# Key and value stage of a four-stage transformer kernel: Pool's clears and bias additions later, constant rows by the scalar engine, last products reordered

## The chip, the cores and the metric

The kernel runs on one core of one Trainium2 chip. The metric is device time in microseconds (us) of one execution. All engines of the core work at once from separate instruction streams and meet at semaphores: PE (TensorE, matrix products, with PEld its weight loads), DVE (VectorE), ACT (ScalarE), POOL (GpSimd, called Pool in the text) and SP (SyncE, which here issues nearly all DMA transfers).

## The reference, cut to what matters

The input x has 8 batches of 256 rows with 512 columns (2,048 rows, which the kernel keeps as 16 tiles of 128 rows). Four blocks are added to it in turn:

```python
x = x + long_convolution(ctx, ctx, layernorm(x))
x = x + quantised_ffn(layernorm(x), w1, b1, w2, b2)
x = x + attention(layernorm(x), ctx, Wq, bq, gq, Wk_img, bk_img, gk_img, Wv_img, bv_img, Wo, bo)
x = x + experts(x)          # 16 routed experts, the best 2 of each row, and 2 shared ones
```

The change lies in the third block's first half. There, with 256 context rows in each batch,

```python
q = rms_norm(x_n @ Wq + bq, gq)          # x_n = layernorm(x)
k = rms_norm(ctx @ Wk_img + bk_img, gk_img)
v = ctx @ Wv_img + bv_img
out = softmax(q k^T / sqrt(32)) v @ Wo + bo          # 16 heads of 32
```

where `rms_norm(y, g) = y * rsqrt(mean(y*y) + 1e-6) * g` over 512 columns. x at this point is the output of the second block, whose last bias (b2) is added late: in the kernel that addition is a step of its own.

## The kernel before, in words

The program is a row of stages, each a `Block` with one hand-written instruction list for each engine; a stage ends when all five engines have come to its end, and the next begins at once on all of them. Four matter here: `stage_ffn` (second block), `stage_keys_values`, `stage_attention`, and the lists of semaphores between them.

`stage_keys_values` works through ten **items** in the order `ITEMS`: keys of batches 0 to 4, queries of batch 0, keys of batch 5, queries of batch 1, keys of batches 6 and 7. An item is one projection of 256 rows to 512 columns, transposed (four chunks of 128 columns by 256 rows), computed as three bf16 products (high by high, high by low, low by high), 48 matmuls in all. Beside the items run sixteen **value tiles** (12 matmuls of 512 columns each), given out by the table `VALUES`: two in each of rounds 1 to 4, one in rounds 5 to 8, two in rounds 9 and 10. In **round i** PE does `products(i)`, `sums(i-1)` (sums of squares of the item before, four matmuls with one column), the value tiles of the round, and `spread(i-1)` (the row scales put on all partitions by a product with a diagonal matrix); in rounds 3 and 5 also `turn_x` (eight transposes of normalised x for a query item). A round with two value tiles is called a two-value round here, the others one-value rounds.

What joins the engines in round i: ACT splits the next source (`split_source(i+1)`), adds the bias and squares the products of item i (`squares`, eight activations), then copies the high parts of values (`values_high`) and of the finished item (`high(i-1)`). Pool folds the squares from four chunks to one (`fold_halves`, two additions) and raises the row variances to the power -1/2 (`row_scale`). DVE does the low part of the next source, `row_variance(i-1)`, the diagonal matrix (`row_scales(i-1)`, line 1179), values with bias and their low parts, `normalise(i-1)`, `low(i-1)`. SP stores each finished key item as three transfers of 256 KB (`store`), or stacks a query item with twelve of 64 KB. So PE's `spread(i-1)` waits for a chain: PE's sums, DVE's variance, Pool's power, DVE's diagonal matrix.

Work that is not part of this chain has been put beside it:

- Pool begins the stage with `clear_retired` (line 98), which sets the 99 semaphores of earlier stages to zero, then fills the constant columns of `v_hi` and `v_lo`, then adds b2 to two x tiles (`add_bias2`, tiles 4 and 5) ahead of the first fold, and to two more after each of the folds 0 to 4.
- The b2 additions of x tiles 0 to 3 stand in `stage_ffn`, on Pool, after rounds 12 to 15 of that stage (line 1048).
- DVE sets the 32 constant rows of `kb` (rows 96 to 127 of the keys of batch 0: zeros, and two rows of ones) with two memsets at the start (lines 1425, 1427), and takes the statistics of x tiles (`x_stats`): 0 to 3 at the start, then two in each of rounds 1 to 6.
- DVE's subtractions that make the low parts of Wq and Wo (`split_weights`, line 1400) stand at the end of rounds 1 and 2.
- In round 10, where nothing is left but values (7,0), (7,1) and item 9, PE does values (7,0), then `spread(9)`, then values (7,1); ACT and DVE have the matching order.
- SP stores item 9 at the end of the stage; nobody waits for that store until the keys of batch 7 are loaded in the attention stage.

At the end of the stage SP waits for all other stores (line 1187 in the profile). The functions follow with their line numbers.

Of the kernel before, what the change touches and what calls it, by code (L numbers as in the profile page):

```python
# [10 lines left out]
F32 = mybir.dt.float32  # L11
# [59 lines left out]
class Kernel:  # L71
# [26 lines left out]
    def clear_retired(self, pool):  # L98

        for s in self.retired:  # L100
            pool.sem_clear(s)
# [682 lines left out]
def stage_ffn(k, scales, b1_parts, b2, ahead, quantised):  # L784
# [3 lines left out]
    with ExitStack() as ctx:  # L788
# [254 lines left out]
        def _(pool):  # L1043
            pool.memset(ahead.rows[:, :], 0.0).then_inc(rows_zeroed, 1)

            def add_bias2(t):
                pool.wait_ge(y_added, t + 2)
                pool.tensor_tensor(tile(t), tile(t), b2[:, :].unsqueeze(1), ALU.add)

# [133 lines left out]
def stage_keys_values(k, ahead, b2, qw, ow, vectors, ks, v_hi, v_lo, x_mean, x_rstd, qs, kb, k_hi, k_lo):  # L1183
# [3 lines left out]
    with ExitStack() as ctx:  # L1187
# [12 lines left out]
        x_var, tmp = (sb(f"kv_{n}", [P, NT], F32) for n in ("xvar", "tmp"))  # L1200
        psW = ctx.enter_context(nc.psum_tensor("ps_kw", [P, P], F32))
# [10 lines left out]
        q_stacked, kb_loaded, kb_set = sem("qst"), sem("kbl"), sem("kbs")  # L1212
        w_high, w_low, rows_turned, vectors_ready, dve_step = (sem(n) for n in ("wh", "wlo", "rt", "ve", "dve"))
        stat_done, x_var_ready, x_rstd_ready, x_biased = (sem(n) for n in ("sd", "xv", "xr", "xb"))
# [13 lines left out]
        FIRST = AHEAD * TPB  # L1228

        @block.gpsimd  # L1230
        def _(pool):
            k.clear_retired(pool)
            pool.memset(v_hi[:, :, :, HD:], 1.0)
            pool.memset(v_lo[:, :, :, HD:], 0.0)

# [8 lines left out]
            def add_bias2(first):  # L1244
                for t in range(first, min(first + 2, NT)):
                    pool.tensor_tensor(k.x[:, t, :], k.x[:, t, :], b2[:, :], ALU.add).then_inc(x_biased, 1)

            add_bias2(FIRST)
            for i in range(N):
# [4 lines left out]
                add_bias2(FIRST + 2 * (i + 1))  # L1254
# [6 lines left out]
        def _(sp):  # L1261
            def store(i):
                b, p = batch(i), i % 2
                done = k.last_stored if i == N - 1 else stacked[p]
                sp.wait_ge(k_low, i + 1)
                for j, part in enumerate((k_hi[p], k_lo[p], k_hi[p])):
                    target = ks[b:b + 1, j * HD:(j + 1) * HD, :, :, :].rearrange("o d h c s -> (o h) d (c s)")
                    sp.dma_start(target, part[:, :, :].rearrange("p c s -> p (c s)")).then_inc(done, 16)
# [10 lines left out]
            for i in range(N):  # L1279
# [14 lines left out]
        def _(act):  # L1294
# [43 lines left out]

            split_source(1)
            act.wait_ge(vectors_ready, 1)  # L1340
            for i in range(N + 1):
# [6 lines left out]
                for n, tile in enumerate(VALUES[i]):  # L1348
                    if n and i == N:
                        high(i - 1, (i - 1) % 2)  # L1350
                    values_high(*tile)
                if 0 < i < N:
                    high(i - 1, (i - 1) % 2)

        @block.vector
        def _(dve):
# [44 lines left out]

            def x_stats(t):
                if t >= FIRST:
                    dve.wait_ge(x_biased, t - FIRST + 1)
                dve.bn_stats(stats[:, t, :], k.x[:, t, :]).then_inc(stat_done, 1)
# [26 lines left out]
            for i in range(1, N + 1):  # L1432
# [9 lines left out]
                if FIRST + 2 * (i - 1) < NT:  # L1442
                    x_stats(FIRST + 2 * (i - 1) + 1)
                if i == N:
                    normalise(i - 1, p)
                    value_low(*tiles[0])
                    low(i - 1, p)
                    value(*tiles[1])
                else:
                    value_low(*tiles[0])  # L1450
                    for tile in tiles[1:]:
                        value(*tile)
                    normalise(i - 1, p)
                for tile in tiles[1:]:
                    value_low(*tile)
                if i < N:
                    low(i - 1, p)
# [1613 lines left out]
```

## Time and profile before

| | us |
|---|---|
| median of three runs | 1165.79 |
| lowest, highest | 1162.44, 1165.82 |
| the profiled execution's own time | 1165.67 |
| its span, first to last instruction | 1163.9 |
| mean granted clock of PE | 0.939 of full |
| `stage_keys_values` in the span | 375.15 to 500.20 |
| PE, DVE, ACT, Pool busy over the span | 91, 76, 60, 52 % |

The profile is one execution, with every instruction's start and duration. A row of the timeline has the start, the duration, the engine, the line of the kernel, the operation, what is written and read, and, in square brackets, how long the engine sat idle before it and whom it waited for. Instructions of one engine overlap by about 0.1 us, so durations add up to a little more than the time that passes; where it matters, distances from start to start are used. The granted clock is 1.00 at PE's full rate (2.4 GHz) and 0.50 at its lower one (1.2 GHz). Waits for PE and DVE in this stage are more telling than the shares over the whole span, since stages have different limits.

### The profile page before, as it was taken

Reading aid. Unit: us, or ns where it says so; the run is one execution under the profiler, and the core shown is the slowest. Engines: PE = TensorE matmul, PEld = TensorE weight load, DVE = VectorE, ACT = ScalarE, POOL = GpSimd, SP = SyncE. Lnnn points to the kernel's source line nnn. Section 1 sums busy time; section 2 is a strip of 40 time slices with the busy share of each in tenths; the row PEclk is TensorE's granted clock in tenths of the full one; section 3 lists DMA queues with packets and bytes.
Section 4 is the critical chain, followed back from the end, with each engine's and each line's share of the span. In section 5 each row is a group of like instructions: output and inputs, shape, how many; then the busy total and the mean of one; then the engine's idle time right before and its main releaser. Section 6 shows DMA issues by size and latency. Waiting matters only on the chain. (4 is left out here: it accounts for less than half of the span.)

```text
span 1163.9 us, 24928 instructions
## 1 busy us (share of the span) xinstructions
PE 1057.2 (91%) x9247; PEld 783.7 (67%) x9247; DVE 881.0 (76%) x1594; ACT 697.4 (60%) x1135; POOL 603.2 (52%) x637
## 2 busy tenths in 40 slices
PE   5999997689997899868999999698998799999997
PEld 5777775634443567547777776497675688888884
DVE  5489999779998988657888888498975455555548
ACT  4564773779985546457888876285454254454531
POOL 4444445434455543348788888222686255555520
PEclk9999999789999999978999999757999799999999
DMA  8573531869885123222222220195697467768879
GB/s 311 165 258 120 163 113 33 156 197 231 231 214 157 67 67 111 76 78 56 54 56 58 56 56 2 51 379 193 168 261 244 146 228 246 240 236 283 314 260 355
DMA packets 133706, 194.62 MB, mean 167 GB/s; under 512 B 67990, under 2 KB 70204, under 8 KB 132792
## 3 DMA queue, kind: packets, MB, share of 16 engines
q1 hardware_dynamic: 117256, 149.45, 42.3%
q0 software_dynamic: 8544, 24.68, 6.7%
q10 hardware_dynamic: 7792, 18.96, 5.2%
q8 instruction: 72, 1.18, 0.4%
q14 instruction: 42, 0.34, 0.1%
HBM read 127.47 MB, written 44.48 MB: 148 GB/s over the span
## 5 line engine op out<-in xcount | busy, mean ns | idle before, releaser
L470 PE MATMUL ps_y<-kv,toep 128*128 128x288 f32 x640 | 157.7, 409 | 4.6 <-DMA toep<-taps_padded 2.4
L470 PEld LDWEIGHTS ps_y<-kv,toep 128*128 128x128 f32 x640 | 122.2, 192 | 39.6 <-DMA toep<-taps_padded 3.5
L1679 POOL TENSOR_TENSOR vw<-at_pf,kw 128x1024 bf16<-128x1024 f32 x64 | 136.5, 2133 | 2.7 <-ACT kw L1739 2.7
L164 POOL TENSOR_TENSOR kv<-kx 128x1024 f32<-128x1024 f32 x32 | 60.6, 1893 | 87.2 <-DVE outT L524 40.2
L2665 POOL DMA_INDIRECT expert_results<-e_yo,target x47 | 70.1, 1491 | 55.5 <-ACT e_yo L2716 55.5
L1735 ACT ACTIVATE at_pf<-ps_st 128x1024 f32<-128x1024 f32 x64 | 65.5, 1024 | 39.7 <-PE ps_st L1875 36.2
L1786 DVE TENSOR_REDUCE at_negmax<-ps_s 128x4 f32<-128x1024 f32 x64 | 78.4, 1224 | 2.5 <-PE ps_s L1836 0.6
L1147 PEld LDWEIGHTS ps_eg<-e_xT,e_w 128*128 128x128 bf16 x1128 | 68.6, 100 | 14.6 <-DVE e_w L2770 2.2
L1147 PE MATMUL ps_eg<-e_xT,e_w 128*128 128x128 bf16 x1128 | 72.6, 222 | 3.7 <-DVE e_xT L2777 3.7
L1147 PE MATMUL ps_eu<-e_xT,e_w 128*128 128x128 bf16 x1128 | 72.8, 222 | 0.0
L2770 DVE COPY e_w<-expert_weights 128x4096 bf16 x47 | 57.7, 1227 | 19.0 <-issue 19.0
L2660 POOL DMA_INDIRECT e_rows<-token_rows,token x45 | 43.5, 968 | 51.2 <-PE ps_ex L2867 45.3
L2783 DVE SCALAR_TENSOR_TENSOR e_y<-ps_eu,e_bias,e_y 128x128 f32<-128x128 f32 x94 | 28.7, 347 | 54.2 <-PE ps_eu L1147 53.5
L1739 ACT ACTIVATE kw<-at_pf 128x1024 bf16<-128x1024 f32 x64 | 67.6, 1057 | 2.0
L1100 PE MATMUL ps_fH<-w1T,f_qaT 128*128 128x512 bf16 x256 | 64.1, 395 | 3.6 <-PEq L636 2.1
L1147 PEld LDWEIGHTS ps_eu<-e_xT,e_w 128*128 128x128 bf16 x1128 | 67.1, 100 | 0.0
L1780 DVE COPY qs<-ps_m 32x256 bf16<-32x256 bf16 x128 | 37.6, 294 | 36.6 <-PE ps_m L1848 33.5
L2732 ACT ACTIVATE e_xT<-ps_ex 128x512 bf16<-128x512 bf16 x47 | 28.1, 597 | 58.8 <-PE ps_ex L2867 58.8
L1116 PE MATMUL ps_fY<-w2T,f_qbT 128*128 128x512 bf16 x256 | 59.4, 387 | 4.2 <-DMA f_qbT<-f_qb 4.2
L494 DVE TENSOR_TENSOR prod<-ps_y,qx 128x1024 f32<-128x1024 f32 x32 | 39.2, 1224 | 25.5 <-ACT ps_y L417 25.5
L1147 PE MATMUL ps_ed<-e_parts,e_yhi 128*128 128x512 bf16 x188 | 55.9, 379 | 0.4 <-DVE e_ylo L2791 0.4
L2725 ACT ACTIVATE e_y<-ps_eg,e_bias 128x128 f32<-128x128 f32 x94 | 29.4, 364 | 39.6 <-PE ps_eg L1147 31.1
(444 smaller groups left out, 3055.4 us busy)
## 6 DMA issues: line engine op xcount, KB each, us to landing
e_parts<-down_parts SPq DMA_DIRECT2D x47, 512.0 KB, 4.6
w_raw<-in_L_ffn_w ACTq DMA_DIRECT2D x32, 512.0 KB, 4.5
toep<-taps_padded SPq DMA_DIRECT2D x32, 256.0 KB, 3.6
f_draw<-in_L_ffn_rw SPq DMA_DIRECT2D x16, 512.0 KB, 4.5
down_parts<-f_dparts SPq DMA_DIRECT2D x16, 512.0 KB, 2.9
expert_weights<-expert_results SPq DMA_DIRECT2D x16, 512.0 KB, 10.7
x_res<-in_x SPq DMA_DIRECT2D x4, 1024.0 KB, 11.9
c_in<-in_ctx SPq DMA_DIRECT2D x4, 1024.0 KB, 14.8
```

Of the source, the lines that this page charges most:

```text
L164: pool.tensor_tensor(pairs[:, :, :, 0:HD0], x[:, :, 0:HD0].unsqueeze(2).broadcast_to([P, ROWS_N, WIDE, HD0]), sliding_rows(x, 0, 1, WIDE), ...
L470: last = pe.matmul(y[:, l * B:(l + 1) * B, :, WIDE - 1:], toep[h % 2][:, (DC - 1 - l + m) * P:(DC - l + m) * P], kv[h % 2][:, m * B:(m + 1 ...
L1100: pe.matmul(psH[:, f, :].rearrange("p (a t) -> p a t", t=P), qaT[p][:, c, :], k.w1T[:, f * DC:(f + 1) * DC, c, :], start=(c == 0), stop=False)
L1116: last = pe.matmul(psY[p][:, :].rearrange("p (a t) -> p a t", t=P), qbT[p][:, c, :], k.w2T[:, :, c, :], start=(c == 0), stop=(c == FC - 1))
L1147: instruction = pe.matmul(out, stationary[a], moving[b], start=first and n == 0, stop=last and n == 2)
L1679: pool.tensor_tensor(pl[u % 4][:, :, :, :], pf[u % 2][:, :, :, :], ph[u % 4][:, :, :, :], ALU.subtract)\
L1735: act.activation(pf[u % 2][:, :, :, :], psT[:, :, :, :], ACT.Exp, scale=SCORE_SCALE).then_inc(exped, 1)
L1739: act.activation(ph[u % 4][:, :, :, :], pf[u % 2][:, :, :, :], ACT.Copy).then_inc(p_high, 1)
L1786: dve.tensor_reduce(negmax[u % 2][:, :].rearrange("p (j q) -> p j q", j=2), psS[:, :, :, :], AX.X, ALU.max, negate=True).then_inc(max_read, 1)
L2660: pool.indirect_dma_start(out=rows[j % 2], out_offset=None, in_=k.scratch["rows"], in_offset=bass.IndirectOffsetOnAxis(ap=token[:, j:j + 1 ...
L2665: pool.indirect_dma_start(out=k.scratch["results"], out_offset=bass.IndirectOffsetOnAxis(ap=target[:, j:j + 1], axis=0), in_=yo[j % 2], in ...
L2770: dve.tensor_copy(w1[j % 2][:, :, :, :].rearrange("p h c f -> p (h c f)"), W[:, bass.ds(e, 1), :, :, :].rearrange("p o h c f -> p (o h c f ...
```

## The change

- `clear_retired` takes a part of the list; Pool clears five parts (20, 20, 20, 20 and 19 semaphores) at the ends of rounds 4 to 8 in place of all 99 at the start.
- Pool's b2 additions move to rounds 2 to 7 (`BIAS_FROM` is 4); DVE's statistics of those tiles move from rounds 1 to 6 to rounds 4 to 9. The b2 additions of tiles 0 to 3 leave Pool in `stage_ffn` and become four additions on DVE at the start of the stage.
- The constant rows of `kb` are written by ACT, one quarter in each of rounds 5 to 8, copied from a column of 32 constants that Pool sets with two small memsets at the start.
- The subtraction for Wo moves from round 2 to round 3 on DVE.
- In round 10 both value tiles come ahead of `spread(9)`, on all three engines.
- The store of item 9 moves from the end of the stage to the front of SP's list in the attention stage, ahead of the copy of the constant rows, the bias loads and the load of batch 1's keys.

```diff
-    def clear_retired(self, pool):
+    def clear_retired(self, pool, n=0, of=1):
-        for s in self.retired:
+        for s in self.retired[n::of]:
             pool.sem_clear(s)
...
 # stage_ffn, gpsimd
                 down_low(n)
-                if n >= NT - AHEAD * TPB:
-                    add_bias2(n - (NT - AHEAD * TPB))
...
 # stage_keys_values
+        CONSTANT_FROM = N - 1 - HC
+        BIAS_FROM = N - (NT - FIRST) // 2
         @block.gpsimd
         def _(pool):
-            k.clear_retired(pool)
-            pool.memset(v_hi[:, :, :, HD:], 1.0)
-            pool.memset(v_lo[:, :, :, HD:], 0.0)
...
-            add_bias2(FIRST)
+            pool.memset(ones_rows[STACK:, :], 0.0).then_inc(rows_set, 1)
+            pool.wait_ge(rows_set, 1)
+            pool.memset(ones_rows[STACK:STACK + 2, :], 1.0).then_inc(rows_set, 1)
+            pool.wait_ge(rows_set, 2)
+            pool.memset(v_hi[:, :, :, HD:], 1.0)
+            pool.memset(v_lo[:, :, :, HD:], 0.0)
             for i in range(N):
                 if i:
                     row_scale(i - 1)
                 pool.wait_ge(squared, (i + 1) * 2 * DC)
                 fold_halves(pool, folded, 2 * i + 2, sq)
-                add_bias2(FIRST + 2 * (i + 1))
+                if BIAS_FROM <= i + 2 < N:
+                    add_bias2(FIRST + 2 * (i + 2 - BIAS_FROM))
+                if BIAS_FROM <= i < N - 1:
+                    k.clear_retired(pool, i - BIAS_FROM, N - 1 - BIAS_FROM)
...
         @block.sync
-            for i in range(N):
+            for i in range(N - 1):
...
         @block.scalar
+            def constant_rows(h):
+                act.activation(kb[STACK:, h, :, :].rearrange("p c s -> p (c s)"),
+                               ones_rows[STACK:, 0:1].broadcast_to([P - STACK, DC * S]), ACT.Copy)
...
-                if 0 < i < N:
+                if 0 < i:
                     high(i - 1, (i - 1) % 2)
+                if 0 <= i - CONSTANT_FROM < HC:
+                    constant_rows(i - CONSTANT_FROM)
...
         @block.vector
-            dve.memset(kb[STACK:, :, :, :], 0.0).then_inc(kb_set, 1)
-            dve.wait_ge(kb_set, 1)
-            dve.memset(kb[STACK:STACK + 2, :, :, :], 1.0).then_inc(kb_set, 1)
+            for t in range(FIRST):
+                first_bias2(t)
...
-                if FIRST + 2 * (i - 1) < NT:
-                    x_stats(FIRST + 2 * (i - 1))
+                if BIAS_FROM <= i < N:
+                    x_stats(FIRST + 2 * (i - BIAS_FROM))
...
-                if i <= 2:
-                    split_weights(i - 1)
+                if i == 1:
+                    split_weights(0)
+                if i == 3:
+                    split_weights(1)
...
         @block.tensor
-                for n, tile in enumerate(VALUES[i]):
-                    if n and i == N:
-                        spread(i - 1)
+                for tile in VALUES[i]:
                     values(*tile)
-                if 0 < i < N:
+                if i:
                     spread(i - 1)
...
 # stage_attention
         @block.sync
         def _(sp):
+            for j, part in enumerate((last_keys[0], last_keys[1], last_keys[0])):
+                target = ks[B - 1:B, j * HD:(j + 1) * HD, :, :, :].rearrange("o d h c s -> (o h) d (c s)")
+                sp.dma_start(target, part[:, :, :].rearrange("p c s -> p (c s)")).then_inc(k.last_stored, 16)
             sp.dma_start(kb[1][STACK:, :, :, :], kb[0][STACK:, :, :, :]).then_inc(ones_copied, 16)
```

How the instructions stand on Pool at the start of the stage, before (`kv_sq` holds the squares, `x_res` is x, `ffn_b` the bias b2; ISA at line 101 is a clear):

```order
L101 ISA x99
L1233 MEMSET v_hi 128x256
L1234 MEMSET v_lo 128x256
L1246 TENSOR_TENSOR x_res<-x_res,ffn_b 128x512 x2
L1171 TENSOR_TENSOR kv_sq<-kv_sq 128x512
L1173 TENSOR_TENSOR kv_sq<-kv_sq 128x256
L1246 TENSOR_TENSOR x_res<-x_res,ffn_b 128x512 x2
```

and in the changed kernel (lines of the changed file):

```order
L1241 MEMSET kv_onesrows 32x1
L1243 MEMSET kv_onesrows 2x1
L1245 MEMSET v_hi 128x256
L1246 MEMSET v_lo 128x256
L1165 TENSOR_TENSOR kv_sq<-kv_sq 128x512
L1167 TENSOR_TENSOR kv_sq<-kv_sq 128x256
L1235 TENSOR_TENSOR kv_r<-kv_v,pow_half 128x2
```

The first fold now has only four memsets ahead of it. The clears and the additions stand in the later rounds; this is Pool in rounds 4 and 5 of the changed kernel:

```order
L1235 TENSOR_TENSOR kv_r<-kv_v,pow_half 128x2
L1165 TENSOR_TENSOR kv_sq<-kv_sq 128x512
L1167 TENSOR_TENSOR kv_sq<-kv_sq 128x256
L1239 TENSOR_TENSOR x_res<-x_res,ffn_b 128x512 x2
L101 ISA x20
```

Each of those rounds had the first three of these rows already, and round 4 the additions too; the additions of rounds 5 to 7 and all the clears are new there. On SP, where the one stage ends and the next begins, the changed order is (before, the first of the three stores of item 9 stood ahead of the two branches, which are the end of the stage, and so did the other two):

```order
L1268 DMA keys_stacked<-kv_khi 4x32x1024
L1181 UNCONDITIONAL_BRANCH
L1625 UNCONDITIONAL_BRANCH
L1629 DMA keys_stacked<-kv_khi 4x32x1024
L1629 DMA keys_stacked<-kv_klo 4x32x1024
L1629 DMA keys_stacked<-kv_khi 4x32x1024
L1630 DMA at_kb<-kb 32x4096
L1633 DMA at_bo<-in_L_xattn_bo 1x512 x2
L1641 DMA at_kb<-keys_stacked 96x4096
```

The copy of the constant rows into the second key buffer and the first load of keys now stand behind three more transfers.

## Rows read from the trace of the kernel before

**Rows 1.** Timeline, PE's sums (L1164) and spreads (L1486), rounds 1 to 4
```profile
389.07 0.61 PE L1164 MATMUL ps_kw<-ones,kv_sq 128*128 128x1 f32 x4 [3.10 <-POOL kv_sq L1173]
...
395.49 0.70 PE L1486 MATMUL ps_r<-kv_diag,ones 128*128 128x256 f32 x2 [0.61 <-DVE kv_diag L1179]
...
401.27 0.50 PE L1164 MATMUL ps_kw<-ones,kv_sq 128*128 128x1 f32 x4
...
408.06 0.70 PE L1486 MATMUL ps_r<-kv_diag,ones 128*128 128x256 f32 x2 [1.09 <-DVE kv_diag L1179]
...
413.84 0.50 PE L1164 MATMUL ps_kw<-ones,kv_sq 128*128 128x1 f32 x4
...
421.56 0.77 PE L1486 MATMUL ps_r<-kv_diag,ones 128*128 128x256 f32 x2 [2.02 <-DVE kv_diag L1179]
...
429.87 0.50 PE L1164 MATMUL ps_kw<-ones,kv_sq 128*128 128x1 f32 x4
...
435.42 0.59 PE L1486 MATMUL ps_r<-kv_diag,ones 128*128 128x256 f32 x2
```

**Rows 2.** Windows, one for each of rounds 5 to 7: stretch, length, busy times, clock
```profile
441.09:450.58 9.49, 9.49 (x76) 7.51 (x75) 7.45 (x15) 5.69 (x12) 3.04 (x3) 1.00 0.46 144
450.58:459.21 8.63, 8.63 (x68) 6.62 (x67) 6.54 (x14) 5.16 (x11) 3.04 (x3) 1.00 0.25 84
459.21:468.36 9.15, 8.89 (x68) 6.55 (x67) 6.51 (x12) 5.94 (x12) 3.04 (x3) 1.00 0.45 119
```

**Rows 3.** Windows of PE alone: length, busy, granted clock
```profile
423.00:424.40 1.40, 1.40 (x8) 0.50 0.26 102
...
385.00:389.00 4.00, 0.97 (x9) 1.00 0.00 0
```

**Rows 4.** Timeline, end of `stage_ffn` on Pool, DVE and PE
```profile
369.81 2.25 POOL L1048 TENSOR_TENSOR x_res<-x_res,ffn_b 128x512 f32<-128x512 f32 x1
...
370.86 3.35 DVE L960 TENSOR_TENSOR vw<-qs,vw 128x2048 bf16<-128x2048 f32 x1
374.13 0.74 DVE L946 SCALAR_TENSOR_TENSOR x_res<-ps_fY,f_out_scale,x_res 128x512 f32<-128x512 f32 x1
...
369.20 3.61 PE L1116 MATMUL ps_fY<-w2T,f_qbT 128*128 128x512 bf16 x16 [1.03 <-DMA f_qbT<-f_qb]
```

**Rows 5.** Timeline, DVE, Wo's low part in round 2
```profile
415.71 2.28 DVE L1400 TENSOR_TENSOR ow<-qs,ow 128x2048 bf16<-128x2048 f32 x1
```

**Rows 6.** Timeline, start of the stage on Pool, ACT and DVE
```profile
382.47 1.24 POOL L1233 MEMSET v_hi<- 128x256 bf16 x1 [10.41 <-issue]
...
386.93 1.27 POOL L1171 TENSOR_TENSOR kv_sq<-kv_sq 128x512 f32<-128x512 f32 x1
...
381.86 0.48 ACT L1320 ACTIVATE kv_sq<-ps_k,vectors 128x256 f32<-128x256 f32 x1
...
380.64 3.47 DVE L1427 MEMSET kb<- 2x4096 bf16 x1 [0.91 <-DVE kb L1425]
```

**Rows 7.** Timeline, DVE's diagonal matrix (two instructions) in rounds 3 and 8
```profile
420.02 1.48 DVE L1179 TENSOR_SCALAR kv_diag<-ident,kv_r 128x128 f32<-128x128 f32 x2 [0.22 <-POOL kv_r L1242]
...
470.93 0.48 DVE L1179 TENSOR_SCALAR kv_diag<-ident,kv_r 128x128 f32<-128x128 f32 x2 [0.82 <-POOL kv_r L1242]
```

**Rows 8.** Timeline, ACT, a copy of 1024 elements for each partition
```profile
467.56 1.04 ACT L1300 ACTIVATE kv_c1hi<-ctxT 128x1024 bf16<-128x1024 f32 x1
```

**Rows 9.** End of the stage: SP's store of item 8, DVE's last row, SP's last wait
```profile
487.62 0.56 SPq L1268 DMA_DIRECT2D keys_stacked<-kv_khi  x1
...
497.16 0.69 DVE L1377 TENSOR_TENSOR v_lo<-kv_vf,v_hi 128x512 bf16<-128x512 f32 x1 [0.70 <-ACT v_hi L1324]
...
SPq L1187 <- DMA keys_stacked<-kv_khi: 2.0, 1, 2.0
```

**Rows 10.** Attention: first use of batch 1's keys; the load's landing (us, last column)
```profile
526.42 0.60 PE L1836 MATMUL ps_s<-at_kb,qs 96*128 96x256 bf16 x4
...
at_kb<-keys_stacked SPq DMA_DIRECT2D x1, 768.0 KB, 9.2
```

More of the change, by code:

```diff
@@ L1244, in add_bias2 @@
             def add_bias2(first):
-                for t in range(first, min(first + 2, NT)):
+                for t in range(first, first + 2):
                     pool.tensor_tensor(k.x[:, t, :], k.x[:, t, :], b2[:, :], ALU.add).then_inc(x_biased, 1)
-            add_bias2(FIRST)
+            pool.memset(ones_rows[STACK:, :], 0.0).then_inc(rows_set, 1)
[4 more added lines that the diff above has]
+            pool.memset(v_lo[:, :, :, HD:], 0.0)
             for i in range(N):
@@ L1267, in store @@
                     target = ks[b:b + 1, j * HD:(j + 1) * HD, :, :, :].rearrange("o d h c s -> (o h) d (c s)")
-                    sp.dma_start(target, part[:, :, :].rearrange("p c s -> p (c s)")).then_inc(done, 16)
+                    sp.dma_start(target, part[:, :, :].rearrange("p c s -> p (c s)")).then_inc(stacked[p], 16)
             def stack(i):
@@ L1404, in x_stats @@
                     dve.wait_ge(x_biased, t - FIRST + 1)
+                else:
+                    dve.wait_ge(first_biased, t + 1)
                 dve.bn_stats(stats[:, t, :], k.x[:, t, :]).then_inc(stat_done, 1)
@@ L1437, in _ @@
                 row_variance(i - 1)
-                if FIRST + 2 * (i - 1) < NT:
-                    x_stats(FIRST + 2 * (i - 1))
+                if BIAS_FROM <= i < N:
+                    x_stats(FIRST + 2 * (i - BIAS_FROM))
                 row_scales(i - 1)
                 value(*tiles[0])
[L1442 to L1453, printed above, removed]
+                if BIAS_FROM <= i < N:
+                    x_stats(FIRST + 2 * (i - BIAS_FROM) + 1)
+                value_low(*tiles[0])
+                for tile in tiles[1:]:
+                    value(*tile)
+                normalise(i - 1, p)
                 for tile in tiles[1:]:
                     value_low(*tile)
-                if i < N:
-                    low(i - 1, p)
+                low(i - 1, p)
                 if is_query(i + 3):
                     normalise_x(batch(i + 3))
-                if i <= 2:
-                    split_weights(i - 1)
+                if i == 1:
+                    split_weights(0)
+                if i == 3:
+                    split_weights(1)
                 if i == N - 1:
@@ L1519, in _ @@
                     sums(i - 1)
-                for n, tile in enumerate(VALUES[i]):
-                    if n and i == N:
-                        spread(i - 1)
+                for tile in VALUES[i]:
                     values(*tile)
-                if 0 < i < N:
+                if i:
                     spread(i - 1)
@@ L1560, in normalise, with stage_attention @@
            .then_inc(self.xn_ready, 1)
-def stage_attention(k, ks, v_hi, v_lo, qw, ow, vectors, x_mean, x_rstd, stats, qs, kb, ahead, front):
+def stage_attention(k, ks, last_keys, v_hi, v_lo, qw, ow, vectors, x_mean, x_rstd, stats, qs, kb, ahead, front):
     nc = k.nc
@@ L2998, in build @@
                                  lambda name: ctx.enter_context(nc.semaphore(name)))
-            stage_attention(k, ks, v_hi, v_lo, qw, ow, k.vectors, x_mean, x_rstd, stats, qs, kb, ahead, front)
+            stage_attention(k, ks, (k_hi[(len(ITEMS) - 1) % 2], k_lo[(len(ITEMS) - 1) % 2]), v_hi, v_lo, qw, ow, k.vectors, x_mean, x_rstd, stats, qs, kb, ahead, front)
             k.retired_stack.close()
```

13 lines of the change are left out of this document (6 added, 7 removed).

## Prediction

> **What bounds the kernel now.** The change touches one stage and the end of the one before, so I read the timeline of that stretch engine by engine, then the waits, and only then the windows round by round. Times below are those of the profiled execution (1165.67 us, 0.12 under the median of the runs shown, so the two can be taken as one).
>
> PE carries the stage. In round 4 nothing holds it: from its sums to its spread it needs 435.42 - 429.87 = 5.55 us, and from that spread to the next sums 441.09 - 435.42 = 5.67 [rows 1, 2]. A one-value round takes 8.63 us, and one with the transposes of x 9.49, so these cost 0.86 [rows 2]. Against this I hold every other stretch of PE, start to start, and call what is over a loss:
>
> - first sums: 3.10 of idle time behind Pool's fold [rows 1];
> - sums to spread in rounds 1, 2 and 3: 6.42, 6.79 and 7.72, so 0.87, 1.24 and 2.17, each time behind DVE's diagonal matrix [rows 1];
> - spread to sums after the first two of them: 5.78 each, so 0.11 twice [rows 1];
> - spread to sums after the third, transposes included: 8.31 - 5.67 - 0.86 = 1.78. Here PE ran at half clock: 0.50 between 423.00 and 424.40 [rows 3]. It fell to 1.2 GHz behind the 2.02 us wait [rows 1], though it had not behind the 3.10 us one, where the window shows 1.00 [rows 3];
> - round 7: 9.15 - 8.63 = 0.52 [rows 2].
>
> Together **9.90 us**. In the early rounds DVE sets the pace: the two spreads that wait for it, in rounds 2 and 3, lie 421.56 - 408.06 = 13.50 us apart, where PE needs 5.55 + 5.67 = 11.22. In the one-value rounds PE and DVE are nearly level.
>
> The end is set by something else. DVE, the last engine to compute, is done at 497.85, but SP waits 2.0 us more for a DMA [rows 9]. It waits for no store of item 9, so this is item 8's, issued at 487.62, when DVE's low part of item 8 was done: it lands about 12.1 us later, and the stage ends at 500.20, 12.6 us after that issue.
>
> **The change part by part.**
>
> *Bias additions out of the FFN stage.* Pool's last one runs from 369.81 to 372.06, and DVE's subtraction under it takes 3.35 us [rows 4], where the same form takes 2.28 with Pool quiet [rows 5]. Without it DVE's last addition, at 374.13, comes 1.07 earlier. It can't gain more than 1.3, since PE's product for it ends at 372.81 [rows 4]. The ends are 0 and 1.3; I take **1.1**, the length that the clean row leaves over.
>
> *Clears, memsets and additions behind the first fold.* Pool's first memset is at 382.47 [rows 6]; the stage began at 375.15, so the 99 clears took 7.3 us, 0.074 each. The squares are ready at 381.86 + 0.48 = 382.34, the fold starts at 386.93 and its sums at 389.07, 2.1 later [rows 1, 6]. With only memsets ahead, the fold starts at 382.4 and ends at 384.5, and PE finishes its products at 385.9. The wait goes: **-3.10**, with no doubt that I can see.
>
> *DVE at the start.* The memsets end at 384.11 [rows 6]; four additions take their place. No row shows this form on DVE; at the price of DVE's own 128x2048 subtraction scaled down (2.28 / 4) they are 2.3 us, at Pool's price twice that. Either is less than the 6 us that the memsets filled. DVE then has the first diagonal matrix 2.6 + 0.5 = 3.1 us after the sums (470.93 against sums at 468.36, and 0.48 [rows 7]), and PE wants it 5.55 after them. Losses of round 1 go: **-0.87 - 0.11**. Pool only writes in its memsets beside these additions. If such a write held DVE up as Pool's addition did in rows 4, that would cost up to the memsets' 2.8 us, and DVE's lead of 2.4 would hide all but 0.4. The Trainium skill (SBUF — State Buffer, Who interferes with whom) says that a DVE instruction with two SBUF inputs is locked out by a Pool instruction that reads SBUF, and not by one that only writes; by this rule the sum has 0 here, by the bound 0.4. No row here shows the pair.
>
> *Rounds 2 to 4.* DVE enters with that lead, so round 2's wait shrinks to what its round is too long by; between 0 and today's 1.24 I take 0.2. From round 2 to 3 the chain of 13.50 loses Wo's subtraction, 2.2 start to start: 11.3 against PE's 11.22, so 0.1 is left of 2.17. Round 4 has that subtraction instead, but PE has the transposes: 0.2. With no wait of 2 us left there, the clock stays up and the 1.78 go. Round 5 is where DVE is late next: its chain is 13.50 - 2.2 - 1.0 (the diagonal matrix without Pool's fold beside it, 0.48 for 1.48 [rows 7]) = 10.3, PE has one value tile and 8.63, so **a new wait of about 1.5**, after what little lead there is. Before, this round had none.
>
> *Constant rows on ACT.* Four copies of 32x1024. The nearest row is a copy of 128x1024 at 1.04 [rows 8]; nothing costs less than 0 and I know no reason for more. In each of rounds 5 to 8 it stands ahead of ACT's next source split, for which DVE waits at the head of its round, and these rounds have no slack. Of the copies of rounds 6 and 7 I take 0.6 each on PE's path, in rounds 7 and 8 (DVE works on its own subtraction meanwhile); round 5's falls on a query item, whose split comes in halves, and round 8 has no split after it. With round 7's present 0.52 that makes waits of 1.1 and 0.6.
>
> *Additions and clears in late rounds.* Pool has 3.04 us busy in a one-value round [rows 2]; two additions (2.5) and 20 clears (1.5) make 7.0 of 8.63. Hidden. Statistics on DVE fill waits for Pool and ACT, which are as long. Hidden; without this cover 0.6 each.
>
> *Last values ahead of the last spread.* PE fills a wait, and DVE may end 0.6 sooner, but item 8's store still ends the stage: **0**. If that store lands sooner for want of item 9's behind it, up to 2.3 are there.
>
> *Item 9's store ahead of the attention stage's first loads.* Batch 1's keys are wanted at 526.42, 26.2 us into the stage. Their load now starts some 3.5 in, behind a store of the same size: 3.5 + 12.1 + 9.2 = 24.8 even if they go one after the other [rows 9, 10]. Cost 0, cover 1.4. One more clear on Pool there: 0.07.
>
> **Sum.** New or left: 0.2 + 0.1 + 0.2 + 1.5 + 1.1 + 0.6 = 3.7. Stage 9.90 - 3.7 = 6.2, FFN 1.1, less 0.1: 7.2 us, so 1165.67 - 7.2 = **1158.5**.
>
> **Rivals.**
>
> *The tail goes too* (item 8's store lands with nothing behind it). For it: SP waits on a DMA and item 9's bytes are in flight then. Against: item 8's were issued first. It gives 1 to 2.3 more, about 1157.
>
> *The clock falls behind a new wait.* For it: 2.02 us was enough once, and four waits of 0.6 to 1.5 remain. Against: 1.09 and even 3.10 did not do it. A fall costs 1.8, so 1160.3, and two 1162.1. The Trainium skill (TensorE: Matmul & The Clock Gate, HAM oscillation) says that waits between bursts of matmuls can bring the low clock back every time; that would make this the likeliest case, and the trace, with one fall behind four waits, bears it out in part.
>
> *The early gain is eaten* because DVE's rounds don't shorten: rounds 2 and 3 keep their losses (1.24 + 2.17 + 1.78 + 0.11 = 5.3, less the 0.3 that I left). Then 2.2 is left, 1163.5: no change. Against it: Wo's subtraction does leave that chain.
>
> *Slower: Pool's moved additions block DVE.* Two additions of 1.24 come to rounds 5 to 7, where DVE has no slack, and the diagonal matrix shows that a collision costs 1.0. If two DVE instructions collide in each of rounds 4 to 8 at 1.0 to 1.25 each, that is 11 us: 1169.5. It decides from 7.2 / 5 = 1.4 us lost in each round. Against it: DVE is not on two-input instructions all the time, and early rounds, which have these additions today, show one such second.
>
> **Chances.** The forecast 0.55, the tail too 0.12, a fall of the clock 0.17, eaten 0.12, slower 0.04. The range reaches from the tail case with shorter late waits, 1154.8, to two falls of the clock, 1162.0. About 0.3% (3.5 us) is what a measurement of this kernel can tell from no change: faster by more, 0.84; within, 0.12; slower, 0.04.
>
> **What would show it.** In the changed profile: PE's first sums right behind its products; the waits of its spreads in rounds 1 to 4 under 0.5 and no half clock there; a wait of 1 to 2 in round 5 and of about 1 in rounds 7 and 8; the FFN's last addition 3.4 to 3.7 us behind the start of PE's last product; SP still waiting for a DMA at the end of the stage. The prediction is wrong if the stage is shorter than today's 125.05 by less than 4 or more than 9 us, or if another stage moves by over 1 us.

## The result and the profile after

| | before | changed |
|---|---|---|
| median of ten runs, us | 1166.92 | 1162.01 |
| lowest, highest | 1162.44, 1171.58 | 1155.04, 1165.39 |
| the profiled execution's own time | 1165.67 | 1161.47 |
| its span | 1163.9 | 1159.7 |
| last FFN product's start to the end of that stage | 5.95 | 6.00 |
| `stage_keys_values`, to attention's first product | 125.09 | 120.52 |
| attention, first product to the router's first transpose | 250.93 | 249.64 |

The ratio is **0.9953**, 95% interval 0.9935 to 0.997: 5.5 us faster, where 7.2 were forecast. The profiled execution is 4.2 faster than that of before. Its changed stage is 4.57 shorter, and what the other stages gained and lost comes to 0.4 the other way. Stages are measured here from PE's first weight load in one to its first product in the next (125.09 before, where the prediction's 125.05 goes from load to load).

PE's sums (L1158) and spreads (L1490) in the changed kernel; they answer to [rows 1]. Columns as there: start, duration, engine, line, operation, and the wait in brackets.

```profile
383.64 0.50 PE L1158 MATMUL ps_kw<-ones,kv_sq 128*128 128x1 f32 x4
...
389.18 0.59 PE L1490 MATMUL ps_r<-kv_diag,ones 128*128 128x256 f32 x2
...
424.69 0.70 PE L1490 MATMUL ps_r<-kv_diag,ones 128*128 128x256 f32 x2 [0.45 <-DVE kv_diag L1173]
430.47 0.51 PE L1158 MATMUL ps_kw<-ones,kv_sq 128*128 128x1 f32 x4
436.06 0.70 PE L1490 MATMUL ps_r<-kv_diag,ones 128*128 128x256 f32 x2 [2.47 <-DVE kv_diag L1173]
...
455.79 0.70 PE L1490 MATMUL ps_r<-kv_diag,ones 128*128 128x256 f32 x2 [1.29 <-DVE kv_diag L1173]
```

The first sums have no wait, and PE's spreads of rounds 1 to 3 have none either. But round 5 waits 2.47, where I had put 1.5, and round 4 has 0.45. What was DVE doing ahead of the spread of round 5? Its timeline there, behind the diagonal matrices of rounds 2 to 4, and Pool's:

```profile
398.99 1.48 DVE L1173 TENSOR_SCALAR kv_diag<-ident,kv_r 128x128 f32<-128x128 f32 x2 [0.81 <-POOL kv_r L1235]
...
410.29 1.55 DVE L1173 TENSOR_SCALAR kv_diag<-ident,kv_r 128x128 f32<-128x128 f32 x2 [0.82 <-POOL kv_r L1235]
...
423.15 1.48 DVE L1173 TENSOR_SCALAR kv_diag<-ident,kv_r 128x128 f32<-128x128 f32 x2 [0.22 <-POOL kv_r L1235]
...
433.48 0.15 DVE L1386 TENSOR_SCALAR kv_v<-ps_kw 128x2 f32<-128x2 f32 x1
433.55 0.68 DVE L1415 BATCH_NORM_STATS2 kv_stats<-x_res 128x6 f32<-128x512 f32 x1
434.46 1.55 DVE L1173 TENSOR_SCALAR kv_diag<-ident,kv_r 128x128 f32<-128x128 f32 x2 [0.22 <-POOL kv_r L1235]
...
433.71 0.71 POOL L1235 TENSOR_TENSOR kv_r<-kv_v,pow_half 128x2 f32<-128x2 f32 x1 [5.58 <-DVE kv_v L1386]
434.66 1.26 POOL L1165 TENSOR_TENSOR kv_sq<-kv_sq 128x512 f32<-128x512 f32 x1 [0.24 <-ACT kv_sq L1320]
```

Pool's fold (434.66 to 435.92) runs beside the diagonal matrix, and that takes 1.55 where a quiet round has 0.48 [rows 7]. This overlap is called the collision from here on. It is there in each of rounds 2 to 5 (1.48, 1.55, 1.48, 1.55). Before, it was there in rounds 1 to 3.

The FFN's end, which answers to [rows 4]: DVE's last subtraction and addition, and PE's last product.

```profile
368.61 2.28 DVE L960 TENSOR_TENSOR vw<-qs,vw 128x2048 bf16<-128x2048 f32 x1
371.95 0.75 DVE L946 SCALAR_TENSOR_TENSOR x_res<-ps_fY,f_out_scale,x_res 128x512 f32<-128x512 f32 x1 [1.07 <-PE ps_fY L1110]
...
366.99 4.92 PE L1110 MATMUL ps_fY<-w2T,f_qbT 128*128 128x512 bf16 x16 [2.76 <-DMA f_qbT<-f_qb]
```

The subtraction is at 2.28, as forecast, but PE's product takes 4.92 where it took 3.61, and DVE waits 1.07 for it. The window of that product (length, PE busy, granted clock, DMA share, GB/s) shows that PE ran part of it at half clock:

```profile
366.90:371.95 5.05, 4.92 (x16) 0.72 0.25 104
```

The stage's end, which answers to [rows 9]: the store of item 8, and SP's last wait.

```profile
481.55 0.56 SPq L1268 DMA_DIRECT2D keys_stacked<-kv_khi  x1
...
SPq L1181 <- DMA keys_stacked<-kv_khi: 9.6, 1, 9.6
```

SP still waits for that DMA, while DVE's last instruction ends at 490.99 and attention's first product starts at 493.51, 11.96 after the issue (before, 12.62).

### The profile page after: what moved, and what is told of

Read it like the earlier page. It is cut to its first block and busy times, and to the rows that moved or that the text cites. A ratio compares the mean times of both kernels' runs of the same rounds, so it can differ in the third digit from the quotient of the medians.

```text
span 1159.7 us, 24854 instructions
## 1 busy us (share of the span) xinstructions
PE 1043.6 (90%) x9168; PEld 778.6 (67%) x9247; DVE 870.4 (75%) x1596; ACT 701.3 (60%) x1139; POOL 599.5 (52%) x635
## 5 line engine op out<-in xcount | busy, mean ns | idle before, releaser
L1740 ACT ACTIVATE at_pf<-ps_st 128x1024 f32<-128x1024 f32 x64 | 65.5, 1024 | 40.6 <-PE ps_st L1880 36.6
L1055 POOL CAST f_dparts<-f_draw 128x1024 bf16<-128x1024 f32 x16 | 17.5, 1095 | 63.9 <-DVE f_qb L938 63.9
```

Source lines behind the costliest of these rows:

```text
L1740: act.activation(pf[u % 2][:, :, :, :], psT[:, :, :, :], ACT.Exp, scale=SCORE_SCALE).then_inc(exped, 1)
```

## The experiments

**Theory at this point.** The waits left on PE are made by one collision: Pool's fold beside DVE's diagonal matrix, 1.0 us in each round in which DVE is late. The rival: they are DVE's plain load, as I had argued. Beside this each part of the change is undone or done alone. Each ratio is to executions of the kernel before that were made beside those of the run. "Stage" alone is `stage_keys_values`.

### Parts of the change, undone or alone

`clears_only`: the kernel before, with only this (and `clear_retired` taking a part of the list, as in the change)

```diff
-            k.clear_retired(pool)
...
                 add_bias2(FIRST + 2 * (i + 1))
+                if 4 <= i < N - 1:
+                    k.clear_retired(pool, i - 4, N - 5)
```

> The kernel before, with one part of the change alone: the 99 clears leave the start of the stage and stand, 20 or 19 at a time, behind Pool's additions and folds of rounds 4 to 8. Bias additions, DVE's memsets and everything else as before. If PE carries the stage, its first sums follow its products (wait 0 for 3.10 before) and this gain is kept to the end: stage shorter by 3.1 to 3.7, time 3 to 4 us under the kernel before (ratio 0.997), the wait of round 3 still about 2 with PE at half clock behind it. If DVE's memsets and its first rounds are level with PE, the wait comes back at the spread of round 1 (over 2.5 there for 0.61), and the stage is shorter by 1 or less. The FFN stage is untouched in both.

Measured: stage 121.53, 3.56 shorter; first sums without a wait; spreads wait 0.47, 1.09 and 2.01 in rounds 1 to 3; `turn_x` behind the last takes 1.45 for 1.04. In the trace it is the first case, PE carries the stage. The time did not follow: ratio 0.9989 (0.9973 to 1.0005), 1.3 us for 3 to 4. So in the traces this one part of the change gives 3.56 of the 4.57 us that all of it gives in this stage; in the time no gain of it is shown.

`ffn_back`: the changed kernel with

```diff
 # stage_ffn, gpsimd
+                if n >= NT - AHEAD * TPB:
+                    add_bias2(n - (NT - AHEAD * TPB))
...
 # stage_keys_values, vector
-            for t in range(FIRST):
-                first_bias2(t)
```

> The changed kernel with the four b2 additions of x tiles 0 to 3 back on Pool in the FFN stage, and no such additions on DVE. Theory 1 (my prediction's term): Pool's last addition stretches DVE's Wv subtraction from 2.28 to about 3.35 and the FFN stage is 1.0 to 1.1 longer than in the changed kernel. Theory 2 (from the trace of the changed kernel): the end of the FFN stage is set by PE, whose last two products run partly at half clock behind waits of 1 to 3 us for a DMA, once in the one and once in the other; the subtraction is stretched but the FFN stage stays within 0.3 of 141.8, unless the fall of the clock moves. In the next stage DVE does its statistics about 2.3 earlier, which only fills waiting time: within 0.3. Theory 2 gives the changed kernel's time (within 1 us), theory 1 gives 1 more.

Measured: the FFN stage takes 141.58 and ends 5.90 after the start of its last product. PE ran that product in 3.61, so this is DVE's end, not PE's. Theory 1 holds for the FFN stage: the next run, which has the changed code, takes 140.56. The keys' stage was not within 0.3: 122.71, with 6.70 us at 0.76 of the clock behind round 5's wait, and with 0.65 more from item 8's store to the end (see `store_back`). The ratio, 0.9994 (0.998 to 1.0008), is 2 to 5 us above those of the two series of the changed kernel, where theory 1 gives 1; these two stages account for about 2, and the rest is open.

`changed_again`: the changed kernel, nothing edited.

> The changed kernel as it is, once more, to see which of its numbers come back. Theory 1 (the fall of the clock is a matter of which wait it follows, and differs between executions of one kernel): PE waits 2.47 at the spread of round 5 again; the clock falls behind it in some executions, as in two variants, and not in others, and the stage is 120.5 without and 122 with it. The FFN stage is 140.3 to 140.6 where its last product runs in 3.6, and 141.8 where it runs in 4.9. Theory 2 (the clock is the same in every execution of a kernel): round 5 at full clock and 4.92 for the last FFN product, as in the first profile. Time against the kernel before: ratio 0.9935 to 0.997, as at first.

```profile
365.79 3.61 PE L1110 MATMUL ps_fY<-w2T,f_qbT 128*128 128x512 bf16 x16 [2.69 <-DMA f_qbT<-f_qb]
...
433.75 1.22 PE L1490 MATMUL ps_r<-kv_diag,ones 128*128 128x256 f32 x2 [2.47 <-DVE kv_diag L1173]
434.76 1.91 PE L1515 MATMUL ps_kx<-ident,kv_xn 128*128 128x128 f32 x8
```

The window of that wait's spread and of what follows it:

```profile
433.75:436.70 2.95, 2.95 (x12) 0.50 0.68 267
```

Theory 1. With the last FFN product at full clock the stage ends 4.90 after its start: 1.05 sooner than before [rows 4]. And behind the same wait of 2.47 PE is at 1.2 GHz here, where the first profile had 1.00; the stage is 121.87, 1.35 longer. The ratio is 0.9974 (0.9956 to 0.9993), which overlaps the first.

`store_back`: the changed kernel with item 9's stores in the stage again (the three in the attention stage are left out).

```diff
-            for i in range(N - 1):
+            for i in range(N):
                 if is_key(i):
                     store(i)
...
```

> The changed kernel with item 9's three transfers back at the end of the stage, as before. If item 8's store was held up before by item 9's behind it, the stage ends again 12.5 to 12.7 after the issue of item 8's store (11.9 in the changed kernel), 0.7 longer, and batch 1's keys in the attention stage come no later or sooner than they are needed: time 0.5 to 0.8 above the changed kernel. If the 0.66 between the two traces was chance, it stays at 11.9 to 12.1 and the time is the same. If having item 9's bytes ahead of the first key load costs something in the attention stage, that stage gets shorter by what it costs (over 0.5).

Measured: attention begins 11.96 after item 8's store, ratio 0.9964 (0.9946 to 0.9982). So item 9's bytes had not held item 8's up; moving the store is worth nothing by itself (stage 121.89, and 121.87 in `changed_again`, both with half clock behind round 5's wait). But it isn't chance either: 12.59 to 12.62 in the kernel before and its three variants and in `ffn_back`, 11.95 to 11.98 in `store_back`, the changed kernel and two more variants of it. The longer one is found where the b2 additions of tiles 0 to 3 stand in the FFN stage, and how the two hang together stays open.

### The collision

`fold_waits` is the changed kernel and `before_fold` the kernel before, each with

```diff
                 pool.wait_ge(squared, (i + 1) * 2 * DC)
+                if i:
+                    pool.wait_ge(diag_ready, i)
                 fold_halves(pool, folded, 2 * i + 2, sq)
```

> The changed kernel with one wait more: Pool starts each round's fold of squares only when DVE's diagonal matrix of that round is done. In the changed kernel the fold runs beside the diagonal matrix in rounds 3, 4 and 5, and that takes 1.48 to 1.55 there for 0.48 elsewhere. Theory 1 (the fold blocks DVE, and what is lost adds up on PE's path): the diagonal matrix takes 0.48 in all rounds, the wait of the spread in round 5 falls from 2.47 to 1.2 to 1.5, that in round 4 from 0.45 to 0, and the stage is 1.5 to 2.0 shorter. Theory 2 (the wait of round 5 is DVE's whole load, not the collision): the collision goes elsewhere (the fold then meets the value addition behind the diagonal matrix) and the stage is shorter by 0.5 at most. Slower if a late fold delays PE's sums: a wait at the sums of any round.

DVE and Pool in round 5 of `fold_waits`, and PE:

```profile
430.51 0.48 DVE L1173 TENSOR_SCALAR kv_diag<-ident,kv_r 128x128 f32<-128x128 f32 x2 [0.22 <-POOL kv_r L1235]
...
432.13 1.28 POOL L1165 TENSOR_TENSOR kv_sq<-kv_sq 128x512 f32<-128x512 f32 x1 [1.66 <-ACT kv_sq L1322]
...
428.43 0.50 PE L1158 MATMUL ps_kw<-ones,kv_sq 128*128 128x1 f32 x4
...
431.39 0.59 PE L1492 MATMUL ps_r<-kv_diag,ones 128*128 128x256 f32 x2
```

The matrix takes 0.48 in every round, the waits of rounds 4 and 5 are gone, and the stage is 116.92: 3.60 less than the best profile of the changed kernel, 4.95 less than the one with the slower clock. Ratio **0.991** (0.9884 to 0.9937), from four executions. Theory 1, but twice its size: I counted one collision on PE's path, and there were four in a row on DVE's. The diagonal matrix of round 5 is ready 58.94 into the stage for 63.02 in the changed kernel, 4.08 = 4 x 1.02 sooner. And the new wait holds Pool back in one round only. The folds of rounds 2 and 3 in `fold_waits`:

```profile
398.68 1.27 POOL L1165 TENSOR_TENSOR kv_sq<-kv_sq 128x512 f32<-128x512 f32 x1 [0.67 <-DVE kv_diag L1173]
...
408.83 1.27 POOL L1165 TENSOR_TENSOR kv_sq<-kv_sq 128x512 f32<-128x512 f32 x1 [0.66 <-ACT kv_sq L1322]
```

In round 2 Pool waits for the matrix, and from round 3 on for ACT's squares alone (1.66 in round 5): once DVE is on time, the matrix is done before the squares are. So the collision feeds itself: DVE is late, the squares are then ready when Pool has raised the variance, the fold starts at once beside the matrix, and DVE is later. In round 2 DVE is late by its own load: its matrix starts 25.97 into the stage in the changed kernel and 25.96 in `fold_waits`.

> The kernel before with one wait more: Pool starts each fold only when DVE's diagonal matrix of that round is done. Before, the two run side by side in rounds 1, 2 and 3, and the matrix takes 1.48 there. Theory 1 (this collision, not Wo's subtraction or the bias additions, makes most of the waits of rounds 1 to 3): 0.48 everywhere, the waits of 0.61, 1.09 and 2.02 fall to 0, under 0.4 and 0.7 to 1.2, the clock stays up, and the stage is 3.5 to 4.7 shorter than 125.05 (3 if the clock falls all the same). Theory 2: the load of DVE makes them, the matrix is shorter but what comes behind it longer, under 1.

Measured: 0.48 in all rounds, waits of 0, 0 and 0.95 in rounds 1 to 3, no half clock behind the last, stage 120.19, 4.90 shorter; ratio 0.9977 (0.996 to 0.9994). Theory 1, slightly above its range. In round 3 0.95 of the 2.02 are left; that they are DVE's load, Wo's subtraction above all, is argued, and no run separates it.

`clears_and_fold`: the kernel before with both of these edits and nothing else.

> The kernel before with the late clears and the wait of Pool's fold for the diagonal matrix, and nothing else of the change: bias additions, DVE's memsets, Wo's subtraction, last values and stores as before. Theory 1 (the two gains add, and the rest of the change brings nothing in this stage): stage 116.5 to 117.3, as short as the changed kernel with the same wait (116.9), first sums without a wait, diagonal matrix 0.48 in all rounds, wait of round 3 about 1 at full clock. FFN stage as before, so the time is 1.1 above the changed kernel with that wait: ratio to before 0.992 to 0.993. Theory 2 (DVE needs the room that its memsets took once the first sums are 3.1 earlier): waits of over 1 at the spreads of rounds 1 and 2, stage 118.5 or more.

Measured: first sums and rounds 1 and 2 without waits, 0.68 in round 3, the spread to the end as before; stage 118.13, above the forecast. Its first sums come 12.28 in, where `clears_only` has 10.62, since PE was at half clock there:

```profile
372.60:376.00 3.40, 3.39 (x16) 0.51 0.58 158
```

With those 1.66 taken off it is 116.47, within the forecast. The ratio, 0.9955 (0.9935 to 0.9975), is above the 0.992 to 0.993 that I expected, and not all of that is explained. By the traces, with those 1.66 taken off, the rest of the change brings nothing in sum in this stage once the collision is gone: 116.47 against the 116.92 of `fold_waits`. That is a sum of gains and losses: the constant rows on ACT alone cost 1.4, as the next runs show.

### The constant rows and the end

`rows_early`: the changed kernel with

```diff
                 for tile in VALUES[i]:
                     values_high(*tile)
+                if 0 <= i - CONSTANT_FROM < HC:
+                    constant_rows(i - CONSTANT_FROM)
                 if 0 < i:
                     high(i - 1, (i - 1) % 2)
-                if 0 <= i - CONSTANT_FROM < HC:
-                    constant_rows(i - CONSTANT_FROM)
```

> The changed kernel with ACT's copy of the constant rows put ahead of the high part of the finished item instead of behind it, where ACT idles 2.5 us in each of rounds 5 to 8. Theory 1 (the copies stand in the way of the next source split, for which DVE waits 0.70 in rounds 7 and 8): the waits of the spreads of rounds 7 and 8 fall from 1.29 and 0.72 to about 0.6 and 0, the stage is 1.2 to 1.5 shorter. Theory 2 (these waits are DVE's own load, and the 0.70 only moves): the same waits within 0.2 and the stage within 0.3.

In the changed kernel, round 7, ACT has the copy (L1340) ahead of the split (L1300) and DVE waits 0.70 for it:

```profile
450.98 1.05 ACT L1340 ACTIVATE kb<-kv_onesrows 32x1024 bf16<-32x1024 f32 x1
452.05 1.06 ACT L1300 ACTIVATE kv_c0hi<-ctxT 128x1024 bf16<-128x1024 f32 x1
...
453.13 1.23 DVE L1366 TENSOR_TENSOR kv_c0lo<-ctxT,kv_c0hi 128x1024 bf16<-128x1024 f32 x1 [0.70 <-ACT kv_c0hi L1300]
```

In `rows_early` the copy stands in ACT's idle time, and the split follows the high part directly:

```profile
446.02 1.05 ACT L1340 ACTIVATE kb<-kv_onesrows 32x1024 bf16<-32x1024 f32 x1
448.60 1.06 ACT L1333 ACTIVATE kv_khi<-kv_u 128x1024 bf16<-128x1024 f32 x1 [1.53 <-DVE kv_u L1396]
449.56 1.04 ACT L1300 ACTIVATE kv_c0hi<-ctxT 128x1024 bf16<-128x1024 f32 x1
```

The waits fall from 1.29 and 0.72 to 0.47 and 0.20 and the stage to 119.10, 1.42 less than 120.52 (round 5 at full clock in both). Theory 1. The ratio, 0.9964 (0.9945 to 0.9982), can't tell it from the changed kernel.

`no_landing_wait`: the changed kernel; item 8's store increments the semaphore of item 9's, and SP waits for both ahead of the load of batch 6.

```diff
+                done = k.last_stored if i == N - 2 else stacked[p]
...
-                sp.wait_ge(stacked[p], stores(N - 2 - p))
+                sp.wait_ge(stacked[p], stores(N - 4 + p))
 # stage_attention
-                    if q == B - 1:
-                        sp.wait_ge(k.last_stored, KEY_INCS)
+                    if q >= B - 2:
+                        sp.wait_ge(k.last_stored, 2 * KEY_INCS)
```

> The changed kernel, but the stage's end no longer waits for item 8's store to land; SP waits for it, with item 9's, ahead of the load of batch 6's keys in the attention stage. Theory 1 (that store sets the end): the stage ends 0.3 behind DVE's last instruction, 2.0 to 2.3 earlier than in the changed kernel, so about 118.3 (or 119.8 with a fall of the clock in round 5), and the time is 2 less, ratio to before about 0.993. Theory 2 (the wait is only moved): the attention stage gets longer by the same amount, at its first loads of keys, and the time stays.

DVE's last instruction of the stage and its first of attention:

```profile
489.64 1.23 DVE L1402 TENSOR_TENSOR kv_klo<-kv_u,kv_khi 128x1024 bf16<-128x1024 f32 x1 [0.52 <-ACT kv_khi L1334]
491.20 0.18 DVE L1750 SCALAR_TENSOR_TENSOR at_xshift<-x_mean,x_rstd 128x16 f32<-128x16 f32 x1 [0.33 <-PEq L1181]
```

0.33 lie between them. The stage is 119.65, 2.22 less than `changed_again` (PE at half clock behind round 5's wait in both). Theory 1 for the stage. Attention took 250.77, which is between the 249.3 to 249.6 of the changed kernel's two profiles and the 250.9 of before, so that some of it is paid back there is neither shown nor excluded: `rows_early`, without this edit, has 251.21. The ratio is 0.9958 (0.9937 to 0.9978).

`best`: the changed kernel with these three edits together.

> The changed kernel with three edits: Pool's fold waits for the diagonal matrix, the constant rows stand ahead of the high part of the finished item, and the stage's end does not wait for item 8's store. If the three gains add, the stage is 116.9 - 1.4 - 2.2 = 113.3 (113 to 113.8), nothing at half clock in it, no wait over 0.5 at a spread but that of round 10, and the time is 12 to 13 under the kernel before (ratio 0.989). If the attention stage pays for the stores in flight, at the first load of batch 1's keys, up to 1.4 of cover goes first, and the ratio stays at 0.990 to 0.991. If the constant rows' gain was covered by DVE's lead once the collisions are gone, the stage is about 114.5.

Measured: stage 113.08, ratio **0.9888** (0.9857 to 0.9918), 13 us under the kernel before. The three gains add in the stage (113.3 expected). The clock over its stretches, first round to the last spread:

```profile
370.80:410.00 39.20, 39.20 (x285) 1.00 0.26 83
410.00:450.00 40.00, 39.53 (x298) 1.00 0.32 101
450.00:477.00 27.00, 25.45 (x168) 1.00 0.29 75
```

`best_values_back`: `best` with the last value tiles on both sides of the last spread again, on PE, ACT and DVE.

> The kernel with those three edits, and with the last two value tiles again on both sides of the last spread, as before. In the changed kernel their order could show nothing, since the stage waited for a DMA 2 us behind DVE. Here DVE sets the end. Theory 1: DVE needs 10.1 from the issue of item 8's store to its last instruction with the old order and 9.4 with the new one, so the stage is 0.6 to 0.8 longer. Theory 2 (the order makes no difference to DVE): the same stage within 0.2. The time alone cannot tell them apart.

Measured: stage 113.69, 0.61 longer, the ratio the same within its interval (0.9843 to 0.9916). Theory 1: the reordering is worth 0.6, and the changed kernel could not show it, because there the stage waited for the DMA.

## Why the prediction was right or wrong

The time (1158.5 forecast, a gain of 7.2; measured 5.5 by the ratio) lay in its range, and faster was right. By its steps:

- **Clears behind the first fold.** 3.10 forecast. The first sums come 10.62 into the stage for 13.88: 3.26; alone, the stage is 3.56 shorter. Right.
- **Bias additions out of the FFN stage.** 1.1 forecast; from the last product's start to the end 4.90 for 5.95, so 1.05. Right, and `ffn_back` gives 5.90 back. In the first profile the term can't be seen, since PE was at half clock in part of the last product. My sign, the last addition 3.4 to 3.7 behind the product's start, failed there (4.96), and was 3.87 in `changed_again` (369.66 after 365.79).
- **DVE at the start.** The four additions took 2.49 together, from 375.24; Pool's memsets run from 373.29 to 375.66, so only 0.42 lie side by side, and nothing is drawn out there. DVE's subtraction ahead of them lies beside the second memset (374.10 to 375.66) for its whole length and takes 1.23 (L1366 at 374.09), as it does with Pool quiet (453.13 in round 7). The Trainium skill (SBUF — State Buffer, Who interferes with whom) says that a Pool instruction that only writes SBUF doesn't lock out a DVE instruction with two SBUF inputs; the trace agrees.
- **Rounds 2 to 4, and the new wait of round 5: the step that failed.** I put 0.2, 0.1, 0.2 and 1.5. Against the lossless distances the changed kernel has 0.22, 0.16, 0.71 and 2.75 (12.24 from sums to sums in round 5 for 9.49). What was wrong is the sentence "a new wait of about 1.5", whose chain had "the diagonal matrix without Pool's fold beside it, 0.48 for 1.48". I read the matrix at 1.48 in round 3 before and took the collision for a feature of that round. It belongs to DVE being late, so it moved on with the lateness, to rounds 4 and 5. I had named the collision only in the rival on the slower side, and blamed the additions for it, where the fold was the cause; `fold_waits` settles that. The additions do draw out what stands beside them on DVE (the low part of values takes 1.07 to 1.22 for 0.69 in rounds 2 to 5), but they do so in `fold_waits` too (1.21 to 1.53 in rounds 2 to 4), and there PE has no wait at the spreads of rounds 1 to 6.
- **The clock.** Forecast at full speed, with a chance of 0.17 for a fall behind a new wait. The first profile of the changed kernel has 1.00 up to the last spread. But of the six profiles with this wait (2.47 or 2.48) in round 5 four have PE at half clock behind it, in whole or in part (`changed_again`, `store_back`, `no_landing_wait`, `ffn_back`), and it costs 1.35 where the pair is cleanest (121.87 and 120.52). So the rival is part of the result in four of these six executions. The Trainium skill (TensorE: Matmul & The Clock Gate, HAM oscillation) says that waits between bursts can bring the low clock back; the traces bear it out for this wait, in four executions and not in two. The waits of its example are longer than this one, so it did not by itself make the fall the likeliest case, as I wrote; still, 0.17 was too little. And "one fall behind four waits" was misread: in the kernel before this stage has a fifth wait, at the last spread, with half clock behind it. It cost nothing, since the store set the end.

```profile
490.60 1.22 PE L1486 MATMUL ps_r<-kv_diag,ones 128*128 128x256 f32 x2 [3.98 <-DVE kv_diag L1179]
...
490.60:494.00 3.40, 3.40 (x9) 0.54 0.26 89
```

- **Constant rows on ACT.** 0.6 and 0.6 forecast; taking them out of the way gave 0.82 and 0.52 of wait, 1.42 of stage. The cost was nearly right (1.2 for 1.42), and avoidable. Rounds 7 and 8 lose 1.55 and 0.98 in all, for 1.1 and 0.6, since round 8 had lost 0.25 before too (468.36 to 477.24 is 8.88).
- **Last values.** 0 forecast, and the wait for the DMA hides it, as I said; without that wait it is 0.61.
- **Item 8's landing.** I left the stage's end at 12.6 behind that store, with up to 2.3 in a rival for want of item 9's bytes behind it. It came 0.66 sooner, and `store_back` shows that those bytes were not the cause.
- **The sum.** PE's losses are 10.15 before, with round 8's 0.25, and 6.42 after: 3.73, and 0.16 before the first sums and 0.66 at the end, make 4.55 of the 4.57 seen. I had 3.7 left where 6.42 were; of the difference 1.25 is round 5, 0.83 rounds 7 and 8, and 0.51 round 4.
- **The sign "another stage moves by over 1 us"** was a poor one. Attention changed by 1.29 in the first profile, and the stretch from the start of the shared experts to the end, whose code is the same, took 367.7 before, 370.9 after and 367.9 in `changed_again`; the stretch ahead of `stage_ffn`, whose code is the same too, took 233.2, 231.2 and 230.1. One profile can't be read to 1 us in stages like these.

## What to carry to other kernels

When an instruction takes three times its usual time, ask in which rounds, and what the other engine does beside it, before you carry either duration into a forecast: a collision that appears only when an engine is late will follow the lateness wherever you push it. An ordering wait on the engine that has time to spare (here one wait ahead of Pool's fold) can cost nothing and free the engine that has none. And a wait that hides a gain today (a store's landing behind the last instruction) is itself the next thing to remove.

## What the hardware showed that was not expected

- Pool's addition of 128x512 holds up DVE's two-instruction scaling of 128x128 by 1.0 (1.48 to 1.55 for 0.48), but Pool's power over 128x12 did not. In the changed kernel's last round they lie on one another and DVE still needs 0.48:

```profile
483.94 2.27 POOL L1231 TENSOR_TENSOR x_rstd<-kv_xvar,pow_half 128x12 f32<-128x12 f32 x1
484.00 0.48 DVE L1173 TENSOR_SCALAR kv_diag<-ident,kv_r 128x128 f32<-128x128 f32 x2 [0.82 <-POOL kv_r L1235]
```

  The Trainium skill (SBUF — State Buffer, Who interferes with whom) says that of a DVE instruction in a two-port mode and a Pool instruction the one that comes first keeps the shared ports to its end, and the other stands still. For the fold the trace agrees: in round 4 its first addition runs from 423.09 to 424.36, and the matrix, issued at 423.15, ends at 424.63. In round 5 the matrix's first instruction is ahead of the fold and takes 0.29, and the second, issued together with the fold at 434.66, takes 1.34. For the power the trace doesn't agree: 2.27 us of it cost DVE nothing, and in round 1 its power over 128x4 (389.33 to 390.36) left DVE's low part of values beside it at 0.70. Why the two differ is open.
- The same wait (2.47) in the same code was followed by half clock in one execution and by full clock in another, and the stage was 1.35 us longer with it.
- The stage ended 11.95 to 11.98 or 12.59 to 12.62 us after the issue of item 8's store (three times 256 KB), by program. In the one program that was profiled twice it was 11.96 and 11.95. Item 9's bytes behind it made no difference (`store_back`). The cause is open.
